# Semaphores released without barriers, block ends without GpSimd's drain, and v's bias products behind q and k, in a two-layer decoder kernel

## The reference

```python
x = x + L0_attn(layernorm(x), ...)   # 16 heads gated, a 4-head and a "meta" attention mixed in
x = x + L0_xattn(layernorm(x), ctx_768, ...)
x = x + L0_ffn(layernorm(x), ...)    # 8 routed gelu experts (top 2), 2 shared
x = x + L1_attn(layernorm(x), ...)   # the quantised attention
x = x + L1_xattn(layernorm(x), ctx_768, ...)
x = x + L1_ffn(layernorm(x), ...)    # 16 routed silu experts (top 2), 1 shared
```

```python
def fake_quant(x):                       # over the whole tensor
    mn, mx = min(x.min(), 0), max(x.max(), 0)
    scale = max((mx - mn) / 255, 1e-8); zp = round(-mn / scale)
    return (clip(round(x / scale) + zp, 0, 255) - zp) * scale
qkv = fake_quant(x) @ fake_quant(qkv_w, axis=0).T + qkv_b    # x over its last axis
attn = softmax(fake_quant(q) @ fake_quant(k).T * scale)
out = attn @ fake_quant(v)
return fake_quant(out) @ fake_quant(proj_w, axis=0).T + proj_b
```

## Time and profile before

| | before |
|---|---|
| median of three runs | 704.65 us |
| the profiled execution: time, span | 704.7 us, 703.0 us |
| mean granted TensorE clock | 0.922 |
| TensorE (PE) busy | 591.0 us, 84% |
| VectorE (DVE) busy | 418.1 us, 59% |
| ScalarE (ACT) busy | 385.2 us, 55% |
| GpSimd (POOL) busy | 95.4 us, 14% |

### The profile page before, as it was taken

The page is one execution under the profiler, slowest core; times in us unless marked ns, Lnnn a source line. Parts: engine busy times, 40 slices in busy tenths (PEclk is TensorE's granted clock), DMA queues, the critical chain, the costliest instruction groups (busy, mean ns, idle before and its releaser), DMA issues. The chain is left out here.

```text
span 703.0 us, 9478 instructions
## 1 busy us (share of the span) xinstructions
PE 591.0 (84%) x3333; PEld 326.4 (46%) x3333; DVE 418.1 (59%) x859; ACT 385.2 (55%) x679; POOL 95.4 (14%) x99
## 2 busy tenths in 40 slices
PE   2379799989998798989999996389888868986878
PEld 1112233322334565879998984011222145445756
DVE  8268677667722824545654236878997185446554
ACT  2246866666665246747664430357898614755421
POOL 7200200110001004500000000597000000011000
PEclk9659999999999998999999996569999889989999
DMA  5333300642063303000000000000000002000000
GB/s 155 90 44 48 91 2 1 88 63 33 12 290 53 38 1 116 1 1 1 1 1 3 13 1 0 0 2 0 2 2 2 1 0 94 5 1 1 1 15 16
DMA packets 14786, 22.69 MB, mean 32 GB/s; under 512 B 3524, under 2 KB 9908, under 8 KB 14356
## 3 DMA queue, kind: packets, MB, share of 16 engines
q1 hardware_dynamic: 12916, 15.54, 11.2%
q10 hardware_dynamic: 1824, 6.55, 2.4%
HBM read 9.99 MB, written 0.52 MB: 15 GB/s over the span
## 5 line engine op out<-in xcount | busy, mean ns | idle before, releaser
L536 DVE TENSOR_REDUCE negmax<-ps 128x2 f32<-128x1024 f32 x96 | 113.9, 1221 | 40.9 <-PE ps L467 40.4
L583 ACT ACTIVATE probs<-ps 128x512 f32<-128x512 f32 x192 | 106.4, 598 | 42.2 <-PE ps L486 40.0
L1829 PEld LDWEIGHTS ps<-experts,hid 128*128 128x128 f32 x640 | 83.6, 193 | 7.0 <-issue 1.0
L583 ACT ACTIVATE probs_q<-ps,score_scale 128x512 f32<-128x512 f32 x128 | 78.2, 688 | 14.6 <-PE ps L486 13.2
L1829 PE MATMUL ps<-experts,hid 128*128 128x128 f32 x640 | 85.1, 277 | 0.0
L536 DVE TENSOR_REDUCE negmax_q<-ps 128x2 f32<-128x1024 f32 x64 | 74.8, 1220 | 6.0 <-PE ps L467 5.5
L864 PE MATMUL ps<-experts,wfc 128*128 128x512 f32 x240 | 78.2, 436 | 0.0
L1912 ACT ACTIVATE hid<-ps 128x512 f32<-128x512 f32 x80 | 47.1, 598 | 50.3 <-PE ps L864 50.2
L467 PE MATMUL ps<-gated 64*128 64x512 bf16 x128 | 29.2, 427 | 20.3 <-DMA gated<-parts 9.2
L2015 DVE SCALAR_TENSOR_TENSOR x_tok<-ps,comb,x_tok 128x128 f32<-128x128 f32 x64 | 18.0, 345 | 46.8 <-PE ps L1829 46.8
L864 PEld LDWEIGHTS ps<-experts,wfc 128*128 128x128 f32 x240 | 41.3, 198 | 5.2 <-issue 1.0
(11 more groups left out here) (368 smaller groups left out, 920.0 us busy)
## 6 DMA issues: line engine op xcount, KB each, us to landing
q_wide<-parts SPq DMA_DIRECT2D x12, 256.0 KB, 5.7
k_wide<-parts SPq DMA_DIRECT2D x12, 256.0 KB, 7.1
experts<-in_L_ffn_Wfc_dram ACTq DMA_DIRECT2D x1, 2560.0 KB, 9.5
experts<-in_L_ffn_Wproj_dram ACTq DMA_DIRECT2D x1, 2560.0 KB, 16.7
gated<-parts SPq DMA_DIRECT2D x18, 128.0 KB, 2.4
qs_x<-crossing SPq DMA_DIRECT2D x5, 256.0 KB, 3.0
w<-in_L_ffn_W_dram SPq DMA_DIRECT2D x1, 1024.0 KB, 5.4
square_weights<-in_squares_dram SPq DMA_DIRECT2D x1, 768.0 KB, 7.2
```

What stands on the lines that cost most here:

```text
L536: nc.vector.tensor_reduce(maxima, scores, AX.X, ALU.max, negate=True).then_inc(self.a_max_done, 1)
L583: nc.scalar.activation(self.probs[0:size, g % self.P_SLOTS, :], ps[0:size, self.B_BANK + g % self.B_SLOTS, :], ACT.Exp, scale=scale).then_ ...
L1829: last = nc.tensor.matmul(K.ps[:, y_bank(g), i * P:(i + 1) * P], hid[:, m % SLOTS, i * P:(i + 1) * P], wproj[:, FT * e + f, :], start=(f = ...
```

## The change

- `recycle` becomes `release`: the same clears on GpSimd, without the two barriers.
- It is called twice instead of once: as the gelu experts' instructions begin (for the semaphores that only the gated attention used), and as the quantised attention's begin (for those of the experts). In both places the call stands between the blocks and behind the allocation of all semaphores of the new block, so that none of them is one that is still to be cleared.
- All five blocks are opened with `no_gpsimd_drain=True`: at the block's end the other engines drain as before and GpSimd doesn't; the barrier is one of semaphores only.
- v's two bias products move behind the products of q and k on TensorE.
- q's range is reduced by halves, each as soon as that half is done, four instructions over 512 columns, and one more combines them.

```diff
-    def recycle(self, keep=()):
+    def release(self, keep):
         done = [n for n in self.made if n not in keep]
-        self.nc.all_engine_barrier()
         self.nc.clear_and_free_semaphores([self.made.pop(n) for n in done])
-        self.nc.all_engine_barrier()
...
+        lasting = set(K.sem.made)
         with ExitStack() as st:
             gated_attention(...)
+        first_sems = set(K.sem.made) - lasting
...
             experts_gelu(K, sb, st, W, A, routing_b, wfc, wproj, h2, ffn0_loaded, nc, Q, X, weights, columns_sb, wide, ft_a, col, row,
-                         (w1, w2, ws1, ws2, xw1, xw2), rest_loaded)
-        K.sem.recycle(keep)
+                         (w1, w2, ws1, ws2, xw1, xw2), rest_loaded, first_sems)
+        experts_sems = set(K.sem.made) - set(keep)
         with ExitStack() as st:
-            quantised_attention(K, sb, st, row, Q, tok_a, ft_a, nc, quant_tiles)
+            quantised_attention(K, sb, st, row, Q, tok_a, ft_a, nc, quant_tiles, experts_sems)
...
# in experts_gelu and in quantised_attention, ahead of the block:
+    K.sem.release(set(K.sem.made) - done_sems)
...
# at all five blocks:
-    with nc.Block() as block:
+    with nc.Block(no_gpsimd_drain=True) as block:
...
# quantised_attention, TensorE:
-            for b in range(NB):
-                nc.tensor.matmul(K.ps[:, BANK[2] + b, :], Q.ones_row[0:1, 0:P],
-                                 Q.bias[0:1, 2, :].unsqueeze(1).broadcast_to([1, TPB, D]), start=True, stop=False,
-                                 skip_group_check=True)
             pe.wait_ge(n["w_high"], 1)
             for a in range(2):
                 for b in range(NB):
...
+            for b in range(NB):
+                nc.tensor.matmul(K.ps[:, BANK[2] + b, :], Q.ones_row[0:1, 0:P],
+                                 Q.bias[0:1, 2, :].unsqueeze(1).broadcast_to([1, TPB, D]), start=True, stop=False,
+                                 skip_group_check=True)
             pe.wait_ge(n["w_v"], 1)
...
# quantised_attention, DVE:
+    q_ends = sb("q_ends", [P, 2, NB], F32, st)
-            for a in range(3):
-                dve.wait_ge((n["q_done"], n["k_done"], n["v_done"])[a], 2)
+            for b in range(NB):
+                dve.wait_ge(n["q_done"], b + 1)
+                product = K.ps[:, BANK[0] + b, :]
+                chain(nc.vector.tensor_reduce(q_ends[:, 0, b:b + 1], product, AX.X, ALU.min, negate=True))
+                chain(nc.vector.tensor_reduce(q_ends[:, 1, b:b + 1], product, AX.X, ALU.max))
+            chain(nc.vector.tensor_reduce(qkv_range.tile[:, 0:2, 0], q_ends[:, :, :], AX.X, ALU.max))
+            for a in range(1, 3):
+                dve.wait_ge((n["k_done"], n["v_done"])[a - 1], 2)
                 last = qkv_range.reduce(chain, K.ps[:, BANK[a]:BANK[a] + 2, :].rearrange("p b t -> p (b t)"), a)
```

More of the change, by code:

```diff
@@ L1743, in experts_gelu @@
 def experts_gelu(K, sb, st, W, A, routing_b, wfc, wproj, h2, ffn0_loaded, nc, Q, X, weights, columns_sb, wide, ft_a, col,
-                 row, late, rest_loaded):
+                 row, late, rest_loaded, done_sems):
     E, NS, FT = 8, 2, 4
@@ L2192, in vector, with quantised_attention @@
         return K.ps[:, self.bank, P:P + n]
-def quantised_attention(K, sb, st, row, Q, tok_a, ft_a, nc, tiles_of_region):
+def quantised_attention(K, sb, st, row, Q, tok_a, ft_a, nc, tiles_of_region, done_sems):
     T = NB * S
@@ L2228, in quantised_attention @@
                          busy=(0, 0, 1))
+    chain_sem = K.sem("q1_chain")
+    K.sem.release(set(K.sem.made) - done_sems)
     def strip_of(ops, which, g, b):
@@ L2295, in _ @@
         def _(dve):
-            chain = Chain(dve, K.sem("q1_chain"))
+            chain = Chain(dve, chain_sem)
             ends = x_range.tile[:, 0:2, 0]
```

## The result

The changed kernel takes 709.5 us (median of nine runs, 708.6 to 723.5), the kernel before 704.5 beside it (nine runs, 704.0 to 708.9). The ratio is 1.0046, 95% interval 1.0024 to 1.0068. Forecast were 704.3 us and a range of 702.0 to 706.0, with 0.89 on no change: the time lies outside, on the slow side. The profiled execution took 708.6 us (span 706.9), against 704.7 (703.0), so the two profiles show 3.9 us of it.

A forecast was written before the change was run, and what follows sets the result against it. DVE's range reductions were taken to bound the quantised block's prologue, with v's TensorE products close behind. Terms 0 + 0 + 0 - 0.41 gave -0.4 us on 704.7: forecast 704.3 us, range 702.0 to 706.0.

The forecast's parts named there:

- Step 1: Recycling boundary ahead of the quantised attention: without two barriers it shrinks to an ordinary one, saving 2.05 us.
- Rival D: Recycling boundary: the 2.33 us belong to starting that block and stay; 706.4 us, chance 0.06.
- Step 2: Added release ahead of the experts: GpSimd's memsets start later, at most 2.05 us, but nothing waits; cost 0.
- Step 3: Block ends without GpSimd's drain: cost taken as 0, with bounds of -1.4 to +1.4 us over five ends.
- Rival C: Block ends: the semaphore-only barrier costs a second 0.28 us at five ends; 705.7 us, chance 0.08.
- Step 4: Quantised block's prologue: DVE starts on v at 438.28 instead of 438.69, 0.41 us earlier, boundary saving included.
- Rival B: Prologue: v's products run wholly at 1.2 GHz behind the bias, 0.7 us slower than before; 705.4 us, chance 0.14.
- B's turning point: Prologue: the kernel turns slower than before if the clock rises after 437.8.
- the later of two guesses at the rise: Prologue: clock rises at 437.14, keeping its distance from TensorE's first work; the other guess kept wall time, 436.79.
- in the same way: Everything behind DVE's six range reductions hangs on their end, so all later work moves by 0.4 us.
- a shift that grows in later stages: Stages behind the prologue: a shift growing where nothing was edited was listed as a sign of being wrong.

The follow-up runs named there:

- e3: Kernel before with only v's two bias products moved behind k; 709.9 us, ratio 1.0044 to the kernel before.
- e4: Kernel before with only the recycling's two barriers taken out and its clears split over two places; 708.4 us, ratio 0.9995.
- e6: Changed kernel plus eight unused filler products on TensorE at the quantised block's head, v's bias still behind k; 704.55 us, ratio 0.9980.
- e10: Changed kernel with all the quantised block's bias products over 128 rows, 127 of them zero, v's still behind k; 706.6 us, ratio 1.0021.
- c1: Changed kernel, nothing altered, profiled once more; 728.7 us, one run.
- e11: Changed kernel with all the quantised block's bias products over 128 rows and v's back at the block's head; 702.7 us, ratio 0.9955.
- e5: Kernel before with only GpSimd's drain left out at all five blocks; 707.2 us, ratio 0.9996.
- e7: Kernel before with seven tiny DVE copies delaying the spreading of the ranges ahead of attention; 709.4 us, ratio 1.0036.
- c2: Changed kernel, nothing altered, profiled once more as a second look; 699.1 us, one run.
- e1: Changed kernel with v's two bias products put back at the quantised block's head; 704.65 us, ratio 0.9986.
- e2: Changed kernel with GpSimd's drain restored at the end of all five blocks; 713.8 us, ratio 1.0106.
- e12: Kernel before with only its three bias products over 128 rows instead of one; 705.1 us, ratio 0.9989.
- c3: Changed kernel with v's bias products back at the block's head, profiled once more; 721.3 us, one run.

## Why the prediction failed, by its own steps

**Step 1, right.** 2.33 became 0.39, predicted 0.28: 1.94 us saved instead of 2.05. e3 keeps 2.33 and e4 has 0.33, so it is this part's doing. Rival D is out.

**Step 2, right.** Timeline of after behind the first boundary, against the earlier trace rows:

```profile
273.46 1.14 ACT L1794 CAST wfc<-experts 128x512 fp32r<-128x512 f32 x2 [0.34 <-PEq L1307]
...
274.01 0.36 POOL L1590 MEMSET f_down<- 128x8 f32 x8 [49.94 <-POOLq L1307]
```
POOL starts 0.55 us behind ScalarE; nothing waited.

**Step 3, right.** The ordinary boundaries, from the last engine's end to the first one's start, are 0.34 to 0.35 us instead of 0.27 to 0.28; forecast was no difference, the bounds 0.28 either way. Rival C, 0.28 more at each end, is out.

**Step 4, wrong, in its clock.** DVE's own order came as worked out: q's halves from 429.86, k done at 435.43 (435.08 forecast). The step that failed starts from "the granted clock rose from half to full at 436.79": afterwards the rise was taken to keep its wall time, or its distance of 8.9 us to TensorE's first work, when that first work changed from bias products to q's. In the profile of after it came at 440.6, 12.0 us after the first product. With it v's products cost 3.78 instead of 2.6, and DVE began v at 440.31 instead of 438.28. Rival B, given 0.14, had this mechanism (v's end at 439.36, DVE at 439.39); the other 0.92 us are small terms: 0.34 at the start of q's second half (429.86 against 429.52; the stages ahead bring 0.2 of it and the boundary 0.11), 0.15 more to k's last product, since that second half too began with a gap of 0.59 and not 0.43, 0.13 between k and the bias, 0.16 in the bias (3.71 against 3.55), 0.14 from v's first product to DVE's start. The text itself put B's turning point at 437.8, and held B unlikely because that lies 0.7 us behind the later of two guesses at the rise. It had one profile and no row for how the rise moves when the work ahead of it changes. It moves much further: 3.7 us behind the block's start in e6, 7.5 in e10, 8.9 in before, 14.5 in after and, in the same kernel as after, 6.4 in c1.

This step alone doesn't carry the miss: B's own time, 705.4 us, lies within the stated range.

What the forecast cited from the Trainium skill, "TensorE: Matmul & The Clock Gate", Part 1 (the HAM clock gate), that the number of slow matmuls differs from run to run, holds here: of v's sixteen records, all were slow in after (421 ns or more), and four in c1, the same kernel, with two more in between.

**The second failure: what follows.** The text let everything behind the six reductions shift "in the same way". The prologue with the boundary accounts for 0.2 - 1.94 + 3.36 - 0.31 = +1.3 of the 3.9 us. The rest, 1.55 + 1.41 less 0.36, is in stages with no edit, at 6 and 3 us more of 1.2 GHz. These stages don't go with the order: e11, the fastest kernel by its median, has an attention of 117.2 us as well, and the last block took 73.4 us in before's profile alone, 74.7 to 74.8 in after, e3, e5 and e11, and 76.1 to 76.5 in the other thirteen. By the medians, e3's 3.1 us are about its prologue; after also saves 1.94 us at the boundary, and that saving shows neither in its time nor in e4's. The forecast had named this as a sign against it ("a shift that grows in later stages"), but gave it no chance.

**The range.** The runs of before, 703.98 to 707.83, were read as scatter around 704.65. They go with the clock: in the sessions before stood mostly near 704, 707 or 709.4 us, at mean granted clocks of 0.922 to 0.925, 0.918 and 0.911. Each run is a draw among such levels. The kernel after stands at 709.2 to 710.2 in seven of its nine runs, at 0.911. A change that moves the start of a stage may move which draw is likely (after and e3 draw a low clock more often than before), and the range had to hold those steps, 3 and 5 us, for an edit worth 0.4.

**What stays open.** What decides between these draws. e7's delay of 0.8 us splits its runs in two groups, e4's shorter boundary does so as well, and c1 and c2 are the same kernel 30 us apart. That v's bias behind k makes the kernel slower is shown by the times of after and e3 against those of before and e1, and that it costs the prologue 0.3 to 3.4 us by after, e2, e3, c1 and c2. Why the clock rose early in c1 and c2 and late in the other three isn't shown, nor whether the moved bias also makes a low clock in the attention likelier.

## What to carry to other kernels

On a stage whose end hangs on TensorE just after a standstill, price its products at both clocks and give the late rise a real chance: an instruction moved off the head of such a stage leaves a hole where the engine's first work was. Before reading a spread of 0.5% as noise, set each run's time against its granted clock: if the times stand in groups, a small change can move a kernel from one group to the next. And where a bias product of one row stands ahead of matmuls that matter, filling it up to 128 rows with zeros costs nothing on TensorE (four records took 3.75 us at 1.2 GHz in e12 as in before) and is worth a trial, though no run here shows a gain in time by that alone.

## What was not expected of the hardware

- One-row products kept TensorE busy for 3.7 us in a stretch of ten busy microseconds without the clock rising (after). With the bias products at the block's head, 128 rows instead of one went with a rise 3.6 us earlier and a fall 3.2 us later (e12 against before); over all profiles the fall is cleanly separated by the rows, the rise only in the kernels with the bias at the head.
- TensorE can be busy 99% of the time at 1.2 GHz for 68 us (c1), 34 us (e1) or 51 us (c3), while other executions of the same instructions stay at or near the full clock. The Trainium skill, "TensorE: Matmul & The Clock Gate", Part 1 (the HAM clock gate), puts the penalty of the ramp up at under 1% of a typical kernel's span. That is no bound for such a stay in the middle of work: c1's attention was 23.5 us longer than e6's, 3.3% of the span, and e1's 14.1 us, 2.0%.
- The start of the kernel has two lengths. The first eight normalising instructions of DVE (L105), in after:

```profile
7.60 3.44 DVE L105 TENSOR_SCALAR xn<-x_tok,mv,std 128x128 f32<-128x128 f32 x4
11.10 4.25 DVE L105 TENSOR_SCALAR xn<-x_tok,mv,std 128x128 f32<-128x128 f32 x4
```
and in c2, the same kernel:

```profile
7.60 1.75 DVE L105 TENSOR_SCALAR xn<-x_tok,mv,std 128x128 f32<-128x128 f32 x4
9.48 2.27 DVE L105 TENSOR_SCALAR xn<-x_tok,mv,std 128x128 f32<-128x128 f32 x4
```
Half the time for the same instructions, 3.7 us less, and the experts start 4.7 us earlier (268.72 against 273.46). None of the other sixteen profiles shows it either: all have the long form. The 4.7 us are about half of what c2's profile is shorter than after's. The cause is open.
